# First layer: blocks of probabilities turned as two 64-row tiles side by side, value products between the two turned steps of a pair

## What is computed

```python
q = q.reshape(b, l, KVH, GROUPS, HD)        # 8 key heads x 4 query heads of 16
scores = einsum('bkgld,bksd->bkgls', q, k) * scale + mask
attn = softmax(scores)
out = einsum('bkgls,bksd->bkgld', attn, v)
```

## Time and profile before

| | us |
|---|---|
| median of 3 runs | 2609.98 (2608.01 to 2610.04) |
| the profiled execution | 2607.51 |
| its span | 2605.7 |
| loop of layer 0, batch 0 | 35.4 to about 284 |
| loop of layer 0, batch 1 | 1330.6 to about 1579 |
| granted clock, mean | 0.995 |

### The profile page before, as it was taken

How to read it: one execution, slowest core, us unless ns; L and a number is a source line. 1 busy time by engine, 2 the same in 40 slices (tenths; PEclk the granted TensorE clock), 3 DMA queues, 4 the chain that set the end, 5 groups by cost and what they waited for, 6 DMA issues and landing times.

```text
span 2605.7 us, 48680 instructions
## 1 busy us (share of the span) xinstructions
PE 2565.0 (98%) x17432; PEld 2123.0 (81%) x17432; DVE 1711.7 (66%) x2600; ACT 1502.2 (58%) x2360; POOL 1310.4 (50%) x746
## 2 busy tenths in 40 slices
PE   7999999999999999999989999999999999999999
PEld 5777788888888888888867777888888888888887
DVE  6999776666656656665269996665666666666541
ACT  5999455555445555545459994555545555554543
POOL 1244246666544666555603433466656446665644
PEclk8999999999999999999999999999999999999999
DMA  8311034354423445442472110335545134544522
GB/s 216 99 51 68 34 82 117 99 130 126 106 68 91 107 105 132 117 113 72 154 169 80 59 61 33 100 99 123 133 99 130 44 100 99 129 127 105 132 70 65
DMA packets 83633, 263.30 MB, mean 101 GB/s; under 512 B 20096, under 2 KB 24336, under 8 KB 77088
## 3 DMA queue, kind: packets, MB, share of 16 engines
q1 hardware_dynamic: 82496, 260.80, 37.6%
q10 hardware_dynamic: 992, 0.52, 0.1%
HBM read 135.39 MB, written 8.40 MB: 55 GB/s over the span
## 4 chain that ended last, share of the span: by engine, by line
PE 86%; issue 4%; POOL 3%; DVE 2%; ACT 2%; DMA 1%; SPq 1%; POOLq 0%; DVEq 0%; ACTq 0%
PE ps_m L1070 20%; PE ps_t L1070 17%; PE ps_s L1070 15%; PE ps_t L1209 6%; PE ps_m L1332 6%; PE ps_t L1332 6%; PE ps_m L1225 5%; PE ps_m L1209 4%; PE ps_s L1192 3%; POOL pT_lo L537 2%; PE ps_m L1265 1%; PE ps_m L1080 1%; SPq L455 1%; POOL v L537 1%; ACT p L815 1%
## 5 line engine op out<-in xcount | busy, mean ns | idle before, releaser
L537 POOL TENSOR_TENSOR pT_lo<-pT_lo,pT_hi 128x1024 fp32r<-128x1024 f32 x220 | 529.0, 2405 | 503.7 <-ACT pT_hi L723 498.9
L723 ACT ACTIVATE pT_hi<-pT_lo 128x1024 fp32r<-128x1024 f32 x224 | 237.7, 1061 | 331.9 <-DMA pT_lo<-pb 331.9
L861 ACT ACTIVATE p<-ps_s,nm 128x1024 f32<-128x1024 f32 x256 | 284.9, 1113 | 205.4 <-DVE nm L1751 204.7
L1748 DVE TENSOR_REDUCE nmx<-ps_s 128x1 f32<-128x1024 f32 x256 | 309.8, 1210 | 121.2 <-PE ps_s L1070 121.2
L1070 PE MATMUL ps_s<-kT,qT 128*128 128x512 f32 x1536 | 384.7, 393 | 1.0 <-ACT p L861 1.0
L1767 DVE STREAM_TRANSPOSE pb<-p 128x1024 f32<-128x1024 f32 x224 | 278.1, 1241 | 112.4 <-ACT p L861 109.0
L1070 PEld LDWEIGHTS ps_s<-kT,qT 128*128 128x128 f32 x1536 | 281.1, 188 | 57.5 <-ACT p L861 2.7
L1672 DVE CUSTOM_DVE_ANT_0 sm<-ps_s,mask 128x1024 f32<-128x1024 f32 x256 | 305.0, 1220 | 28.1 <-PE ps_s L1192 24.3
L815 ACT ACTIVATE p<-sm,nm 128x1024 f32<-128x1024 f32 x256 | 290.9, 1141 | 8.1 <-DVE nm L1672 7.2
L1070 PE MATMUL ps_t<-ctxT,wa 128*128 128x512 f32 x1080 | 256.0, 390 | 0.0
L1070 PE MATMUL ps_m<-hT,wa 128*128 128x512 f32 x1008 | 243.9, 393 | 2.4 <-POOL wa L537 1.6
(11 more groups left out here) (181 smaller groups left out, 4590.5 us busy)
## 6 DMA issues: line engine op xcount, KB each, us to landing
pT_lo<-pb SPq DMA_DIRECT2D x896, 128.0 KB, 2.3
stg_qk<-in_wqk SPq DMA_DIRECT2D x40, 1024.0 KB, 7.5
stg_vo<-in_wo SPq DMA_DIRECT2D x48, 512.0 KB, 3.5
wob<-in_wo SPq DMA_DIRECT2D x32, 512.0 KB, 3.6
stg_vo<-in_wv SPq DMA_DIRECT2D x32, 512.0 KB, 3.6
q_stack<-scr_q SPq DMA_DIRECT2D x48, 128.0 KB, 4.2
st_ctx<-in_ctxT SPq DMA_DIRECT2D x8, 512.0 KB, 6.1
scr_q<-parts SPq DMA_DIRECT2D x8, 512.0 KB, 6.7
```

The lines of the kernel that those rows point to most:

```text
L537: return nc.gpsimd.tensor_tensor(out, x, f32(hi), ALU.subtract)
L723: return nc.scalar.activation(out, in_, ACT.Copy)
L861: nc.scalar.activation(p[t % 2][:], ps_s[t % 2][:], ACT.Exp, bias=nm[:, i:i + 1], scale=SCALE1, accum_out=sums[:, i:i + 1]).then_inc(exp_d ...
L1748: nc.vector.tensor_reduce(nmx[:, i:i + 1], ps_s[t % 2][:], AX.X, ALU.max, negate=True)\
```

## The change

`turned0` no longer turns blocks of 128 queries by 128 keys. It turns two blocks of 64 queries by 128 keys, one in the row tile at rows 0, one at rows 64, alternating, for each of eight blocks of keys. Half q now holds the queries 64 q to 64 q + 63 of all eight blocks of keys, where it held all queries of four blocks of keys. Both banks' waits now stand ahead of all turns, followed by an `apart()`. The copies of ScalarE and VectorE write the corresponding halves of `pt0`: eight runs of 64 elements instead of one run of 512. In TensorE's order the value products stand between `turned0(t-1)` and `turned0(t)`. In ScalarE's order `exp0(t+1)` stands between its two copies.

```diff
@@ ScalarE, copied0 and its loop
-                    copy(pt0[t % RING][:, 4 * q:4 * q + 4, :], half0(t, q)[:].rearrange("p (s n) -> p s n", s=4))\
+                    copy(pt0[t % RING][:, :, TILE * q:TILE * q + TILE], half0(t, q)[:].rearrange("p (s n) -> p s n", s=ST))\
                         .then_inc(t0_copied[q], 1)
...
                 for t in range(1, STEPS0, 2):
                     copied0(t - 1, 0)
+                    if t + 2 < STEPS0:
+                        exp0(t + 1)
                     copied0(t, 0)
                     if t + 2 < STEPS0:
-                        exp0(t + 1)
                         exp0(t + 2)
@@ TensorE, turned0
-                        for s in range(4):
-                            st = 4 * q + s
-                            mm = nc.tensor.transpose(half0(t, q)[:, s * P:(s + 1) * P],
-                                                     p0[t % 2][:, st * P:(st + 1) * P], ident[:])
-                        mm.then_inc(t0_filled[q], 1)
+                    apart()
+                    for st in range(ST):
+                        for q in range(2):
+                            rows = slice(TILE * q, TILE * q + TILE)
+                            mm = nc.tensor.transpose(half0(t, q)[:, st * TILE:(st + 1) * TILE],
+                                                     p0[t % 2][rows, st * P:(st + 1) * P], ident[rows, rows])
+                            if st == ST - 1:
+                                mm.then_inc(t0_filled[q], 1)
@@ TensorE, the loop over pairs
                     turned0(t - 1)
-                    turned0(t)
                     if t >= GROUPS:
                         for i in (t % GROUPS - 1, t % GROUPS):
                             values0(t // GROUPS * GROUPS - GROUPS, i)
+                    turned0(t)
@@ VectorE, copied0
-                    nc.vector.tensor_copy(pt0[t % RING][:, 4 * q:4 * q + 4, :],
-                                          half0(t, q)[:].rearrange("p (s n) -> p s n", s=4)).then_inc(t0_copied[q], 1)
+                    nc.vector.tensor_copy(pt0[t % RING][:, :, TILE * q:TILE * q + TILE],
+                                          half0(t, q)[:].rearrange("p (s n) -> p s n", s=ST)).then_inc(t0_copied[q], 1)
```

## The result

| | before | after |
|---|---|---|
| median, us | 2608.74 (8 runs, 2607.20 to 2612.38) | 2615.75 (8 runs, 2614.30 to 2625.28) |
| ratio, with its 95% interval | | 1.0032 [1.0020, 1.0044] |
| profiled execution; its span | 2607.51; 2605.7 | 2616.33; 2614.3 |
| granted clock, mean | 0.995 | 0.989 |

The change costs 7 us by the medians and 8 by the ratio, where 9 were to be gained: a small loss, and clear of the noise. The page after, first line of busy times, stands beside the earlier trace rows: TensorE is busy for 67 us less in 2048 more products, and still the end comes later. The second line is the queue that brings instructions (packets, MB, share); before it had 98 packets.

The account below looks back on a forecast made before the run. TensorE, busy 98%, was taken to bound the kernel, with VectorE's floor of 14.31 us a unit next. Thirty units at 0.28 give 8.4, with start 9.0: profiled 2607.5 to 2598.5, median 2601 us; range 2589 to 2618.

Parts of the forecast that it names:

- The step for two tiles: TensorE's turns, one block of 128 keys: 0.070 us taken, low bound 0.057, high bound 0.218.
- the copies: ScalarE's and VectorE's copies into eight runs of 64 elements: cost 0 at both ends.
- the wait for `aT`: Once per unit, first products wait for VectorE's aT; VectorE loses 0.24 plus 0.08, 0.32 us, between 0.23 and 0.4.
- The unit of 14.63: New steady-loop unit of 8 steps: VectorE's 14.31 plus 0.32 us for aT, against 14.91 before.
- VectorE's floor: Maxima, copies, reciprocal and aT start to start: 14.31 us a unit, 3.58 a pair; saving at most 0.60 per unit.
- the gain per unit: Steady loop: 0.28 us less per unit, 8.4 us for 2 x 15 units.
- The first rival: Inside each turned step the tiles' weight loads go one after the other: step 0.110, +33 us, 2643; chance 0.13.
- there I take 0 to 0.5 us a batch: First unit of a batch, under bank order 0, 1 alone, part half clock and turns waiting for VectorE's copy.
- loop (a): T(even) needs the previous odd step's banks: 2.2 + 15 x step, 3.2 us at 0.070, under 3.58.
- TensorE's slack: In the new loop TensorE idles about 0.7 us a pair, hiding the added semaphore bumps and `apart`.
- scores to first turn: TensorE's seam after the scores: 0.55 us without change of tile shape; 0.1 more if the 0.36 pause stays.
- the third rival: Clock: a fifth of the loop at half clock from TensorE's idle time, +40 us, 2650; chance 0.05.

Follow-up runs that it names:

- e_banks: Changed kernel with the rotation over three banks from the first step, VectorE's low_part(5) moved before the loop; 2608.79 us, ratio 0.9990.
- b_bsn: Kernel before (whole turns, old orders) with the edits of e_banks, e_spread and e_norm; 2603.97 us, ratio 0.9979.
- e_order: Kernel before, whole turns, with only the two new orders on TensorE and ScalarE; 2635.98 us, ratio 1.0095.
- e_spread: Changed kernel with the loads of acc and the weights spread over later value steps, x_res and row left in place; 2616.93 us, ratio 1.0027.
- r_after: Changed kernel run once more with no edit; 2615.52 us.
- e_late2: Changed kernel with x_res and row loaded after the fourth value step, the rest after the sixth, GpSimd's rows two units later; 2611.10 us, ratio 1.0009.
- f_bsn: Changed kernel with the edits of e_banks, e_spread and e_norm together; 2589.22 us, ratio 0.9926.
- e_norm: Changed kernel with aT made before both maxima on VectorE and the copy to rb before the second exp on ScalarE; 2601.88 us, ratio 0.9968.
- e_warm: Changed kernel with 30 useless turns ahead of the first scores and 22 between the first two; 2617.04 us, ratio 1.0025.
- e_late: Changed kernel with loads of x, w0o, rows and wob held back until five parts of the value products are done; 2629.1 us, ratio 1.0061.
- f_late2: Kernel f_bsn with the later loads of e_late2; 2589.52 us, ratio 0.9929.

## Why the prediction was wrong

**Right.** The step for two tiles (0.070 taken, 0.062 measured, bounds 0.057 and 0.218); that loads of two row tiles run side by side; the copies (0.69 and 0.68, unchanged); that the wait for `aT` is the one that ends last, once per unit. The unit of 14.63 was measured as 14.62, but this close it is luck. VectorE's floor was taken as 14.31 and is 14.20, the wait as 0.32 beyond it and is 0.42: two errors of 0.1 that cancel. Likewise the gain per unit (0.34 for 0.28): the kernel before was read from one clean unit of 14.91, and its mean is 14.96. The first rival, loads one after another, is refuted by the starts.

The Trainium skill ("TensorE: Matmul & The Clock Gate", LDWEIGHTS) has a load cost its columns at 1.2 a nanosecond, 0.107 us for the 128 of a tile. Two such loads fit here into one step of 0.062, so the rate is not that of these fp32 turns; that rows don't matter for a load the measurements leave standing.

**Wrong: the first unit of a batch.** The step that failed is "there I take 0 to 0.5 us a batch", counted as a gain. The prediction named the limits there (bank order 0, 1 alone, half clock, turns waiting for VectorE's copy), and did not work them out with its own loop (a): that loop had three banks in it. With two, a turned step waits for both copies of the step before it, and VectorE's copy stands behind two maxima in its list. Before, the first four blocks needed only ScalarE's bank and ran while VectorE was still busy. The first four pairs cost 4.1 us instead of giving up to 1. With three banks they take 32.3 (`e_banks`) instead of 40.3, and with whole turns 32.9 (`b_bsn`) instead of 36.2: two banks cost the new form 8 us and the old one 3.3, and the difference is the loss.

**Wrong: nothing was priced for more instructions.** The change adds 53032 - 48680 = 4352 of them, and the prediction counted their durations only. The packets of the instruction queue (16 KB each) grow from 98 to 114. The stop inside a run of products has no wait of the program behind it, its length follows the load on the DMA queues (1.0 and 3.2 us at the same instruction), and none of the three kernels with whole turns shows one (before, `e_order`, `b_bsn`). The traces also hold the time of every packet of that queue, and these tie the stop to it (us from the span's start):

| run | packet of the instruction queue | the stop ends | behind the packet's end |
|---|---|---|---|
| changed kernel | 73.70 to 74.78 | 76.22 | 1.44 |
| changed kernel, second batch | 1373.22 to 1374.28 | 1375.76 | 1.48 |
| `e_banks` | 77.63 to 78.70 | 80.17 | 1.47 |
| `e_spread` | 74.69 to 75.77 | 77.12 | 1.35 |
| `r_after` | 64.64 to 65.63 | 67.23 | 1.60 |
| `e_late2` | 70.89 to 72.49 | 73.78 | 1.29 |
| `f_bsn`, second batch | 1360.22 to 1361.33 | 1362.54 | 1.21 |

The traces have 35 stops of over 0.35 us inside runs of like products or turns with no wait of the program, in 9 of the 11 profiles with row tiles. Every one ends 1.2 to 1.6 us behind the end of such a packet, though the packets come 3 to 11 us apart. So TensorE stood for its instructions. In the kernel before the packet was as late (64.72, then 75.31, against 63.60 and 73.70), but TensorE began 290 entries of the trace in between, and 382 in the changed kernel: smaller instructions use up a packet sooner. With the half clock behind it the eight pairs are 4.9 and 3.7 us over their steady 29.2.

**Wrong: the end of a batch.** The moved step's last place was not looked at. After the last pair nothing is left to cover the copies of the last turned step: +1.2 us in the first batch, +2.5 in the second, where the clock halved for 3.4 us as well.

**Half right: TensorE's slack and the clock.** Scores and turns now both use row tiles, and the prediction let the pause between them go for that. It stayed, and is 0.47 instead of 0.36; scores to first turn take 0.77 where 0.55 was taken. In `e_norm` TensorE idles 0.36 a pair, about half of the 0.7 forecast; VectorE's floor hid the difference. The prediction set the third rival aside because pauses would stay far below 2.6 us. But a wait of 1.17 us for `aT` was enough in some units: in `e_late2` (timeline, then the window)

```profile
1495.94 1.48 PEld L1238 LDWEIGHTS ps_m<-pt,v 128*32 128x32 f32 x32 [1.17 <-DVE aT L1705]
```
```profile
1496.00:1499.30 3.30, 3.30 (x52) 2.78 (x52) 1.86 (x4) 1.30 (x3) 0.00 (x0) 0.50 0.00 0
```

Such a fall costs 1.35 us: two pairs take 5.21 + 3.72 where they take 4.04 + 3.54 otherwise. Such falls, in the loop or at its end and away from the stops of 3 us, are in all seven profiles that have this wait: one in the changed kernel's first profile (at the end), two each in `e_banks` and `e_warm`, three each in `r_after`, `e_spread` and `e_late2`, five in `e_late`. All 19 stand at the end of a wait for `aT` of 0.85 to 1.17 us. There are none in `e_norm`, `f_bsn` and `f_late2`, which do not have it. The price of 40 us was far too high, the mechanism real. What the prediction cites beside this rival, that turns do not count as activity for the clock, is not so in the rows of `e_warm`.

**The floor.** `e_norm` runs at 14.20 a unit, with pairs of 3.48, 3.55, 3.48 and 3.68, the reciprocal costing 0.07 and not 0.15.

**Open.** Why a packet that comes late is followed by 1.2 to 1.6 us more before TensorE goes on. And some 2 us of the total at the start and between the batches, beyond the lines that the change touches, were not traced.

## What to carry to other kernels

A steady loop can be predicted to 0.1 us a unit from its rows, and the change still lose by its edges. So work out the first and the last turn of a loop with their own resources (here two banks instead of three), and count how often the loop is entered. Where a change splits work into more and smaller instructions, look at the packets of the instruction queue beside the engine's own rows. An edit that frees one engine pays only once the wait that it leaves on the next is moved: here `aT` ahead of two maxima, a few lines, was worth more than the turns, and was worth it only with them.

## What the runs showed that was not expected

Two fp32 turns of 64 rows in two row tiles proceed at 0.062 us for both, with 128 columns of weights loaded for each. TensorE can stand for 0.5 to 3 us between two instructions without a wait, longer while DMA moves 411 GB/s, in places that change from one execution to the next, and goes on 1.2 to 1.6 us behind a packet of the instruction queue. The clock fell to its half level at the end of waits as short as 0.85 us, and 30 and 22 turns of no use at the loop's start held it up only until the first stop of 3 us.
